# A second, channel-major load of x in place of the transposes on TensorE, in a fused layer norm, RWKV and feed-forward kernel

## The reference

```python
xn = layernorm(x)                       # over the channels, eps 1e-5
shifted = xn moved one token on, zero at a sequence's start
xr, xk, xv = mu * xn + (1 - mu) * shifted        # three vectors mu_r, mu_k, mu_v
r, k, v = xr @ Wr.T, xk @ Wk.T, xv @ Wv.T        # 512 x 512 each
wkv = wkv_v4(k, v, w, u)                # a recurrence along the tokens, per channel
att = (sigmoid(r) * wkv) @ Wo.T
hidden = silu(xn @ W1.T) * (xn @ W3.T)  # 2048 wide
ffn = fwht(hidden) @ W2.T               # Walsh-Hadamard along the 2048, then 2048 -> 512
out = x + att + ffn
```

## Time and profile before

| | |
|---|---|
| median of 3 runs | 2900.99 us (2900.93 to 2901.68) |
| profiled execution, span from first to last instruction | 2900.1 us |
| granted TensorE clock, mean | 0.995 |
| PE busy | 2850.4 us, 98% |
| DVE, ACT, POOL busy | 2026.9, 943.5, 152.8 us |
| DMA, mean busy share of 16 engines' span | 52.8%, 177 GB/s |

### The profile page before, as it was taken

One profiled execution on the slowest core, in us unless ns is written; L12 is line 12 of the kernel. 1 busy time (PEld: TensorE's weight loads), 2 busy tenths in 40 slices (PEclk: granted clock), 3 DMA queues, 4 the chain that ended last, 5 costly groups with the idle time before them and its releaser, 6 DMA issues.

```text
span 2900.1 us, 36707 instructions
## 1 busy us (share of the span) xinstructions
PE 2850.4 (98%) x12576; PEld 2342.9 (81%) x12576; DVE 2026.9 (70%) x2902; ACT 943.5 (33%) x1619; POOL 152.8 (5%) x100
## 2 busy tenths in 40 slices
PE   4999999999999999999999999999999999999999
PEld 2788888888888888888888888888888888888887
DVE  8996867667676676767758676576766757667575
ACT  3544233242332424224242232423324242242421
POOL 7351000000000000000000000000000000000000
PEclk8999999999999999999999999999999999999999
DMA  3677545455454555545455454555545555455554
GB/s 129 231 269 272 177 166 187 151 182 174 166 182 158 179 168 184 170 154 193 160 183 171 159 190 151 188 167 173 180 157 177 180 164 184 152 188 166 167 170 149
DMA packets 157042, 512.34 MB, mean 177 GB/s; under 512 B 15440, under 2 KB 15696, under 8 KB 157008
## 3 DMA queue, kind: packets, MB, share of 16 engines
q1 hardware_dynamic: 157008, 511.91, 52.8%
HBM read 463.61 MB, written 48.23 MB: 176 GB/s over the span
## 4 chain that ended last, share of the span: by engine, by line
PE 95%; DVE 4%; ACT 0%; issue 0%; DMA 0%; POOL 0%; SPq 0%; ACTq 0%; DVEq 0%
PE bank L470 16%; PE bank L468 16%; PE bank L469 16%; PE acc L481 10%; PE acc L483 10%; PE acc L482 10%; PE bank L441 6%; PE bank L443 6%; PE bank L442 6%; PE bank L412 1%; DVE fly L363 1%; DVE ring L801 0%; DVE mixf L709 0%; DVE mix L716 0%; DVE fly L355 0%; DVE pab L747 0%
## 5 line engine op out<-in xcount | busy, mean ns | idle before, releaser
L468 PE MATMUL bank<-xs,ring 128*128 128x512 f32 x1564 | 609.3, 390 | 4.7 <-POOL ring L385 4.7
L470 PE MATMUL bank<-xs,ring 128*128 128x512 f32 x1564 | 609.1, 389 | 0.0
L469 PE MATMUL bank<-xs,ring 128*128 128x512 f32 x1564 | 608.4, 389 | 0.0
L832 DVE SCALAR_TENSOR_TENSOR hidf<-hidf,bank 128x512 f32<-128x512 f32 x256 | 175.9, 687 | 336.5 <-ACT hidf L615 334.4
L481 PE MATMUL acc<-ring,hid 128*128 128x512 f32 x1024 | 402.0, 393 | 0.3 <-POOL ring L385 0.3
L483 PE MATMUL acc<-ring,hid 128*128 128x512 f32 x1024 | 399.1, 390 | 0.0
L482 PE MATMUL acc<-ring,hid 128*128 128x512 f32 x1024 | 398.4, 389 | 0.0
L628 ACT ACTIVATE hid<-hidf 128x512 fp32r<-128x512 f32 x256 | 162.1, 633 | 592.8 <-DVE hidf L835 592.8
L468 PEld LDWEIGHTS bank<-xs,ring 128*128 128x128 f32 x1564 | 293.6, 188 | 67.6 <-DVE hidf L835 3.9
L470 PEld LDWEIGHTS bank<-xs,ring 128*128 128x128 f32 x1564 | 293.6, 188 | 61.6
L469 PEld LDWEIGHTS bank<-xs,ring 128*128 128x128 f32 x1564 | 293.6, 188 | 61.3
(11 more groups left out here) (98 smaller groups left out, 4187.5 us busy)
## 6 DMA issues: line engine op xcount, KB each, us to landing
ring<-split_units SPq DMA_DIRECT2D x780, 512.0 KB, 3.3
split_units<-ring SPq DMA_DIRECT2D x60, 512.0 KB, 3.4
res<-x SPq DMA_DIRECT2D x16, 1024.0 KB, 6.8
xn<-x SPq DMA_DIRECT2D x15, 1024.0 KB, 7.4
out<-res SPq DMA_DIRECT2D x15, 1024.0 KB, 5.9
raw<-units_w SPq DMA_DIRECT2D x32, 256.0 KB, 3.9
fly<-units_w SPq DMA_DIRECT2D x4, 1024.0 KB, 11.3
resident<-split_units SPq DMA_DIRECT2D x8, 512.0 KB, 6.4
```

Of the source, the lines that this page charges most:

```text
L468: pe.matmul(banks[b + n][:, :], w[:, 0, col], xs[:, 0, kt, :], start=kt == 0, stop=False)
L469: pe.matmul(banks[b + n][:, :], w[:, 1, col], xs[:, 0, kt, :], start=False, stop=False)
L470: last = pe.matmul(banks[b + n][:, :], w[:, 0, col], xs[:, 1, kt, :], start=False, stop=kt == KT - 1)
L832: g = step(dve.scalar_tensor_tensor(f[:, :], f[:, :], 1.0, banks[b][:, :], ALU.add, ALU.mult))
```

## The change

x is passed a second time as `x_t`, laid out on the host with the channels first in every chunk. SP loads it straight into `xt` (1 MB for a chunk, destination one column in). The tokens' means and inverse roots are in the partitions of the tokens, so they are stored in a small DRAM buffer `token_rows` (128 partitions, two rows of four numbers, 16 bytes each) and loaded back, broadcast to all 128 partitions (512 KB), into `tok`, which is the memory of the third `mix` buffer. DVE then subtracts the mean and multiplies by the inverse root, each on two channel tiles at once (128x1024, `centre` and `scale`). The normalising in token order, the transposes, their copies, and the waits for them are gone. The load of x in token order stays for the statistics (now four consecutive tokens to a partition) and that of the residual stays as it was. `shift` (the one column from the chunk before) moves from j = 11 to the end of the k, v, r part.

```diff
-FLIP_AT = 12
+STATS_AT = 1
+CENTRE_AT = 9
...
 def load_x(t):
-    wait(sp, xt_psum, t - 1, KT)
-    sp.dma_start(xn[:, :, :], rows(x, t)).then_inc(x_loaded, 16)
+    wait(sp, var_ready, t - 1, 1)
+    sp.dma_start(xrow[:, :, :], x[bass.ds(t * N, N), :].rearrange("(p t) c -> p t c", t=TT))\
+        .then_inc(x_loaded, 16)
+def load_x_t(t):
+    wait(sp, shift_ready, t, 1)
+    sp.dma_start(xt[:, :, 1:N + 1], x_t[bass.ds(t * N, N), :].rearrange("(p k) n -> p k n", k=KT))\
+        .then_inc(xt_loaded, 16)
+def store_token_rows(t):
+    wait(sp, rstd_ready, t, 1)
+    sp.dma_start(token_rows.rearrange("a (p t) -> p a t", t=TT), mean_rstd[:, :, :])\
+        .then_inc(tok_stored, 16)
+def load_token_rows(t):
+    wait(sp, tok_stored, t, 16)
+    sp.dma_start(tok[:, :, :], token_rows.partition_broadcast(P)).then_inc(tok_loaded, 16)
...
                     if unit == ("w1", 1):
                         load_x(1)
+                    if unit == ("w1", 3):
+                        load_x_t(1)
+                    if unit == ("w1", 8):
+                        store_token_rows(1)
+                    if unit == ("w1", 9):
+                        load_token_rows(1)
...
                     if n == 4 and not is_last(t):
                         load_x(t + 1)
+                    if n == 13 and not is_last(t):
+                        load_x_t(t + 1)
+                    if n == 30 and not is_last(t):
+                        store_token_rows(t + 1)
+                    if n == 33 and not is_last(t):
+                        load_token_rows(t + 1)
...
-                    if j in (FLIP_AT, FLIP_AT + 1) and not is_last(t):
-                        wait(pe, hid_full, t, j)
-                        transposes(t + 1, (0, 1) if j == FLIP_AT else (2, 3), 2 - 2 * (j % 2))
...
-            copy_xt(0, (0, 1), 2)
-            copy_xt(0, (2, 3), 0)
+            wait(act, rstd_ready, 0, 1)
+            act.dma_start(token_rows.rearrange("a (p t) -> p a t", t=TT), mean_rstd[:, :, :])\
+                .then_inc(tok_stored, 16)
+            wait(act, tok_stored, 0, 16)
+            act.dma_start(tok[:, :, :], token_rows.partition_broadcast(P)).then_inc(tok_loaded, 16)
             mix_first(0, 0)
...
+            def centre(t, pair):
+                if pair == 0:
+                    wait(dve, xt_loaded, t, 16)
+                    wait(dve, tok_loaded, t, 16)
+                x2 = xt[:, 2 * pair:2 * pair + 2, 1:N + 1]
+                return step(dve.tensor_tensor(x2, x2, tok[:, 0:1, :].broadcast_to([P, 2, N]), ALU.subtract))
...
-                        if TT + 3 <= j < 2 * TT + 3:
-                            normalise(t + 1, j - TT - 3)
-                        if j == 2 * TT + 3:
-                            shift(t + 1)
+                        if j in (CENTRE_AT, CENTRE_AT + 2):
+                            at["centred"] = centre(t + 1, (j - CENTRE_AT) // 2)
+                        if j in (CENTRE_AT + 1, CENTRE_AT + 3):
+                            scale(t + 1, (j - CENTRE_AT) // 2, base, at["centred"])
```

More of the change, by code:

```diff
@@ L92, in units_of_step, with build @@
               else min(4 * u[1] + 5, FT)))]
-def build(nc, x, w_units, vectors, hadamard, identity, out):
+def build(nc, x, x_t, w_units, vectors, hadamard, out):
     f32, f32r = mybir.dt.float32, mybir.dt.float32r
@@ L100, in build @@
     split = nc.dram_tensor("split_units", [NU, P, 2 * C], f32, kind="Internal").ap()
+    token_rows = nc.dram_tensor("token_rows", [2, N], f32, kind="Internal").ap()
     ctx = ExitStack()
@@ L124, in build @@
         var_eps = sb("var_eps", [P, TT])
-        rstd = sb("rstd", [P, TT])
+        mean_rstd = sb("mean_rstd", [P, 2, TT])
         banks = [ctx.enter_context(nc.psum_tensor(f"bank{i}", [P, N], f32)) for i in range(4)]
         acc = [ctx.enter_context(nc.psum_tensor(f"acc{i}", [P, C], f32)) for i in range(TT)]
-        xn = sb("xn", [P, TT, C])
+        xrow = sb("xrow", [P, TT, C])
         xt = sb("xt", [P, KT, N + 1])
@@ L133, in build @@
         mix = [sb(f"mix{i}", [P, 2, N], f32r) for i in range(MIX_AHEAD)]
+        tok = mix[MIX_AHEAD - 1][:, :, :].bitcast(f32)
         kvr = sb("kvr", [P, 3, KT, N])
@@ L324, in _ @@
             for tt in range(TT):
-                sp.dma_start(xn[:, tt, :], x[tt * P:(tt + 1) * P, :]).then_inc(x0_loaded[tt], 16)
+                sp.dma_start(xrow[:, tt, :], x[0:N, :].rearrange("(p t) c -> p t c", t=TT)[:, tt, :])\
+                    .then_inc(x0_loaded[tt], 16)
             sp.dma_start(vec[:, :, :], vectors).then_inc(vec_loaded, 16)
-            sp.dma_start(ident[:, :], identity).then_inc(ident_loaded, 16)
+            sp.dma_start(xt[:, :, 1:N + 1], x_t[0:N, :].rearrange("(p k) n -> p k n", k=KT)).then_inc(xt_loaded, 16)
             sp.dma_start(had[:, :], hadamard).then_inc(had_loaded, 16)
@@ L371, in inverse_root @@
                 wait(pool, var_ready, t, 1)
-                pool.tensor_tensor(rstd[:, :], var_eps[:, :], half[:, :], ALU.pow).then_inc(rstd_ready, 1)
+                wait(pool, tok_stored, t - 1, 16)
+                pool.tensor_tensor(mean_rstd[:, 1, :], var_eps[:, :], half[:, :], ALU.pow).then_inc(rstd_ready, 1)
             pool.wait_ge(const_made, 1)
@@ L405, in weights @@
                 return ring[n % RING]
[L407 to L424, removed]
             def rkv_item(t, n):
@@ L460, in up @@
                     wait(pe, hid_full, t, j - 1)
-                if j in (FLIP_AT + 1, FLIP_AT + 2) and not is_last(t):
-                    wait(pe, xt_copied, t + 1, 2 * (j - FLIP_AT))
                 for n, name in enumerate(("w1", "w3")):
@@ L531, in mix_first @@
                 if n == 0:
-                    wait(act, xt_copied, t, KT)
                     wait(act, shift_ready, t, 1)
+                if q == 0 and kt % 2 == 0:
+                    wait(act, xt_ready, t, kt // 2 + 1)
                 wait(act, mix_lo, t, n + 1 - MIX_AHEAD)
@@ L555, in evacuate @@
                                    scale=0.5 if q == 2 else 1.0).then_inc(kvr_ready, 1)
[L557 to L563, removed]
             def split_hi(unit):
@@ L688, in token_stats, with add_eps, scale @@
                     wait(dve, x_loaded, t - 1, 16)
-                return step(dve.bn_stats(stats[:, tt, :], xn[:, tt, :]))
+                return step(dve.bn_stats(stats[:, tt, :], xrow[:, tt, :]))
             def token_mean_var(tt):
                 return step(dve.bn_aggr(mean_var[:, tt, :], stats[:, tt, :]))
-            def add_eps(base, ready):
+            def add_eps(t, base, ready):
                 wait_step(base, ready)
+                wait(dve, tok_stored, t - 1, 16)
+                copied = step(dve.tensor_copy(mean_rstd[:, 0, :], mean_var[:, :, 0]))
+                wait_step(base, copied)
                 dve.tensor_scalar(var_eps[:, :], mean_var[:, :, 1], EPS, None, ALU.add).then_inc(var_ready, 1)
[L699 to L702, removed]
+            def centre(t, pair):
[4 more added lines that the diff above has]
+                return step(dve.tensor_tensor(x2, x2, tok[:, 0:1, :].broadcast_to([P, 2, N]), ALU.subtract))
+            def scale(t, pair, base, centred):
+                wait_step(base, centred)
+                x2 = xt[:, 2 * pair:2 * pair + 2, 1:N + 1]
+                dve.tensor_tensor(x2, x2, tok[:, 1:2, :].broadcast_to([P, 2, N]), ALU.mult).then_inc(xt_ready, 1)
             def mix_item(t, n):
@@ L826, in chunk @@
                     dve.wait_ge(fly_dve, 8)
+                if not is_last(t):
+                    wait(dve, mix_full, t, 12)
+                    wait(dve, xs_lo, t, KT)
+                    shift(t + 1)
                 wkv(t, base, 0, 0, at)
@@ L881, in _ @@
                 done = token_mean_var(tt)
-            add_eps(0, done)
+            add_eps(0, 0, done)
             dve.wait_ge(vec_loaded, 16)
@@ L886, in _ @@
             dve.wait_ge(decay_made, 2)
-            for tt in range(TT):
-                normalise(0, tt)
             dve.memset(xt[:, :, 0], 0.0).then_inc(shift_ready, 1)
+            for pair in range(2):
+                scale(0, pair, 0, centre(0, pair))
             steps[1] = steps[0]
@@ L900, in _ @@
             over_chunks(dve, chunk)
-STEPS = 15 * KT + FT + 2 * TT
+STEPS = 15 * KT + FT + 2 * TT + 3
 def _square_units(w):
@@ L934 @@
         "x": np.ascontiguousarray(np.asarray(L0_attn_x).reshape(B * T, C)),
+        "x_t": np.ascontiguousarray(np.asarray(L0_attn_x).reshape(CHUNKS, N, KT, P).transpose(0, 3, 2, 1))
+               .reshape(B * T, C),
         "vectors": np.ascontiguousarray(vectors),
         "hadamard": np.ascontiguousarray(hadamard, np.float32),
-        "identity": np.eye(P, dtype=np.float32),
     } | {f"units_{n}": w for n, w in weights.items()}
@@ L943 @@
     out = nc.dram_tensor("out", (B * T, C), mybir.dt.float32, kind="ExternalOutput").ap()
-    build(nc, ap["x"], {n: ap[f"units_{n}"] for n in weights}, ap["vectors"], ap["hadamard"],
-          ap["identity"], out)
```

(1 more changed line is left out.)

25 lines of the change are left out of this document (10 added, 15 removed).

## The result

The changed kernel takes 2897.1 us (median of 20 runs, 2895.15 to 2899.42), the kernel before 2901.55 (2900.72 to 2901.93): a ratio of 0.9985, 95% interval 0.9979 to 0.9991. The prediction was 2881.6 with a range of 2875 to 2892. It is faster by 4.4 us, where 20 were forecast. The runs of the changed kernel also spread over 4.3 us, those of before over 1.2.

A forecast was written before the change was run, and what follows sets the result against it. PE was taken to bound the kernel after about 176 us: span 2900.1 - 27.7 (transposes) + 7.1 (start) + 1.2 (chunk 0) = 2880.7, with runs about 0.9 above span: 2881.6 us, range 2875 to 2892.

The forecast's parts named there:

- the sign of being wrong in kind: On PE's timeline: only waits of PE in each chunk would show the forecast wrong in kind; none were expected after chunk 0.
- What bounds the kernel: PE, waiting for nobody from 175.97 to 2900 us: removing its transposes in chunks 1 to 15 saves 27.7 us.
- the predicted 174.81 us a chunk: PE's period in the looped chunks without transposes, down from 176.66 us.
- DVE, "price nothing": DVE in each chunk: 4.7 us of work instead of 2.3 is covered and costs nothing; without cover, 36 us.
- SP's queue, "nothing": SP's added DMAs in each chunk: x_t, token store and token load are all hidden and cost nothing.
- the rival that starves the ring: SP's weight loads in each chunk: the off-boundary x_t load is slow and makes w1 late, 2925 us; chance 0.04.
- The start, S = 7.1: Before DVE's first mix: token store 3.6 us, load 5.3 and DVE work 4.7 delay it by 7.1 us, carried whole.
- The first two rivals: Token trip at the start: idle-queue prices, S = 3.6, 2876.9 us, chance 0.17; behind the whole backlog, S = 15.7, 2890.2, 0.19.
- the fit that the prediction set beside its sum: Token trip at the start: 2.0 us plus bytes by 436 GB/s gives 2.0 and 3.2 us, S about 3.4.
- Chunk 0, 1.2 us: Rest of chunk 0: x_t of chunk 1 queues among split-weight stores while POOL releases PE; between 0 and 2.7, taken as 1.2.
- Two steps of cover: nothing: Late chunk 0, after 180 us: `centre` and `scale` for chunk 1 beside POOL's work cost nothing, with two steps of cover.

The follow-up runs named there:

- e11: Kernel before without the transposes and copies of chunks 1 to 15, plus 9 idle PE matmuls and a wait ahead of chunk 0: 2874.26 us, ratio 0.9906.
- e5: Changed kernel plus 17 idle matmuls on PE and 60 one-column memsets on DVE, all ahead of chunk 0: 2887.51 us, ratio 0.9950.
- e3: Changed kernel with chunk 0 prepared as before (normalise, transposes, copies; no token trip ahead of it), later chunks as changed: 2891.91 us, ratio 0.9969.
- e4: Changed kernel, but SP issues the later W2 loads and raw weights only after chunk 0's token rows have landed: 2891.33 us, ratio 0.9965.
- e9: Changed kernel with chunk 0 prepared as before, plus 9 idle matmuls on PE and 60 memsets on DVE: 2875.54 us, ratio 0.9910.
- e10: Changed kernel with chunk 0's token trip kept but ahead of SP's backlog, and PE's and DVE's loops both moved: 2882.89 us, ratio 0.9936.
- e7: Kernel before, nothing changed but 40 idle matmuls more on PE inside chunk 0: 2910.78 us, ratio 1.0032.
- e8: Kernel before with 25 one-column memsets more on DVE ahead of chunk 0: 2907.54 us, ratio 1.0020.
- e2: Kernel before without the transposes and copies for chunks 1 to 15, which work on chunk 0's x; no token trip: 2889.0 us, ratio 0.9958.

## Why the prediction was wrong

The miss lies mostly in the loop (8.8 us) and partly at the start (5.1 us). The prediction named waits of PE in each chunk as the sign of being wrong in kind, and that sign came.

- **What bounds the kernel.** "Whatever is taken from its program in chunks 1 to 15 is taken from the time" is the step that failed. It holds for the instructions' execution: e11 and e5 have the predicted 174.81 us a chunk. It does not hold for the program, which PE has to load too. Taking 16 matmuls out of the loop and 32 out ahead of it moved the loop to a place where it is loaded anew in each pass, 9 pieces of 16 KB in each of 13 returns (117 more packets on q8). In the kernel before, no packet of q8 falls between 407 and 2733 us. No rival had this, and no row of before that I quoted spoke of it, although the page's part 3 lists those queues.
- **DVE, "price nothing".** Right for the work: no step waits for `centre` or `scale` in the loop. Wrong for the code: seven instructions more in the loop and five ahead of it make DVE load 5 pieces of 8 KB in each pass and stand idle for 3.3 us at its start (43.4 us in 13). Together the two cost 14 x 0.63 = 8.8 us in the profiled run, 9.6 by the medians.
- **SP's queue, "nothing".** Right: x_t lands in 7.2 us (median), the token load in 4.2, the token store in 4.4, and in e5 PE has no wait after 250 us. Loads of 1 MB of x took 7.4 before, so the off-boundary destination does not slow x_t, and the rival that starves the ring is dead.
- **The start, S = 7.1.** Right in mechanism, the term too small: it measured 12.2. Store 6.5 instead of 3.6, load 6.6 instead of 5.3, and the inverse root itself ready at 10.0 instead of 9.2. The four DVE operations took 4.8 (predicted 4.7), and the delay was carried whole (e3: 11.7 of 12.2 came back). The first two rivals bracket it: idle prices would have been 3.6, the whole backlog 15.7. ACT's load landed at 23.27 while the DMA engines ran at 386 GB/s and above up to 24 us. That is near the end of the backlog; e4 shows that both transfers shorten when it is gone. They neither shared from the start nor stood behind all of it: each waited nearly 4 us behind SP's packets and then shared. The Trainium skill ("DMA: Bandwidth & Descriptors", Queues, rings and completion order) has the queues take turns packet by packet. The stretch from 20 to 22 us agrees; the 3.3 us before it, with 639 packets of q1 on 16 engines and none of q10, fit only if one turn is some 30 to 40 of these packets long, and no run shows that it is. The Trainium skill gives the fit that the prediction set beside its sum (same page, Anatomy of one DMA) for DMAs issued by GpSimd; ACT's took 6.5 us each here where it gives 2.0 and 3.2.
- **Chunk 0, 1.2 us.** The size was right (1.4 measured), but by luck, for the cause was wrong: the waits for POOL did not grow (4.7 before, 3.3 after). PE waited 1.12 us for DVE's product at 224.71. DVE had worked without a pause since 186.7 us, and in that stretch stand three of the four longer operations, one of them, a `centre` beside POOL's work, of 2.31 us instead of 1.22. The kernels that have these operations show the same wait of 1.1 us (e3, e5, e9, e10); e11, without them, does not. "Two steps of cover: nothing" is refuted there.

## What to carry to other kernels

A looped program has a place, and taking instructions away can move it: after each edit, compare the packets of the `instruction` queues with those of the kernel before, and look at the first instruction of a pass for idle time whose releaser is "issue". If they have grown, move the loop with a few harmless instructions in an idle stretch before judging the edit; on this kernel that is worth between 6 and 15 us, as much as half of the edit itself. A round trip through DRAM at the start, where the queues are full, is paid in full: keep the old preparation for the first chunk, which gives back 11.7 us here.

## What the runs showed that I had not expected

- Idle matmuls and memsets in an idle stretch changed the time of everything after them: +9.0 us (e7), +5.8 (e8), -9.6 (e5), -14.7 (e11 against e2).
- Where PE's loop is reloaded the time also scatters: 4.3 us between 20 runs of the changed kernel, 7 us between 4 of e2, against 0.4 to 0.9 us between 4 runs of each of e5, e9, e10 and e11, and 1.2 between 20 of the kernel before.
- A store of 4 KB in pieces of 16 bytes took 4.1 to 4.4 us (median) in the loop and 6.5 us at the start, longer than the 3.3 us of a load of 512 KB.
